# Attention of a four-layer kernel: values and turned probabilities as rounded parts and rests, multiplied in three passes

## The reference

```python
q = (hidden_states @ Wq.T).reshape(b, s, NH, HD).transpose(0, 2, 1, 3)     # NH = 16, HD = 128
k = (hidden_states @ Wk.T).reshape(b, s, NKV, HD).transpose(0, 2, 1, 3)    # NKV = 4
v = (hidden_states @ Wv.T).reshape(b, s, NKV, HD).transpose(0, 2, 1, 3)
scores = jnp.einsum('bhqd,bhkd->bhqk', qf, kf)
scores = jnp.where(causal, scores, neg)
attn = jax.nn.softmax(scores, axis=-1).astype(v.dtype)
out = jnp.einsum('bhqk,bhkd->bhqd', attn, v_rep)
return out.transpose(0, 2, 1, 3).reshape(b, s, NH * HD) @ Wo.T + bo
```

## Time and profile before

| | |
|---|---|
| median of 3 executions | 1227.35 us |
| the profiled execution | 1228.41 us, its span 1226.7 us |
| TensorE busy | 1124.7 us (92% of the span) |
| weight loads, beside it | 963.5 us (79%) |
| VectorE, ScalarE, GpSimd busy | 852.9, 637.3, 211.1 us |
| attention's main loop | about 33 to 469 us of the span |
| granted TensorE clock, mean of the span | 0.927 |

### The profile page before, as it was taken

The page is one execution under the profiler, slowest core; times in us unless marked ns, Lnnn a source line. Parts: engine busy times, 40 slices in busy tenths (PEclk is TensorE's granted clock), DMA queues, the critical chain, the costliest instruction groups (busy, mean ns, idle before and its releaser), DMA issues. The chain is left out here.

```text
span 1226.7 us, 26372 instructions
## 1 busy us (share of the span) xinstructions
PE 1124.7 (92%) x9980; PEld 963.5 (79%) x9980; DVE 852.9 (70%) x2427; ACT 637.3 (52%) x1596; POOL 211.1 (17%) x245
## 2 busy tenths in 40 slices
PE   3999999999999998999999999578799889898888
PEld 2799899889989987888888898456577667776767
DVE  4677567647856776667766757798889779777343
ACT  4654444444444443553444434456788688665341
POOL 0422132222222222430000000200220121021100
PEclk9999999999999998999999999678798798867789
DMA  9020000000000003001000000100000000000034
GB/s 311 2 70 2 1 1 1 1 1 1 2 1 1 1 1 95 1 1 28 1 1 1 1 1 30 57 30 3 32 30 3 31 31 30 3 2 3 25 94 141
DMA packets 26701, 32.90 MB, mean 27 GB/s; under 512 B 4960, under 2 KB 21968, under 8 KB 26576
## 3 DMA queue, kind: packets, MB, share of 16 engines
q1 hardware_dynamic: 24400, 29.12, 7.5%
q10 hardware_dynamic: 2176, 2.10, 0.5%
HBM read 29.04 MB, written 2.17 MB: 25 GB/s over the span
## 5 line engine op out<-in xcount | busy, mean ns | idle before, releaser
L365 DVE TENSOR_TENSOR a_ps<-a_ps,causal 128x256 f32<-128x256 f32 x128 | 54.7, 427 | 100.9 <-PE a_ps L635 100.9
L1537 PE MATMUL b_ps<-ln_high,b_high 128*128 128x512 f32 x256 | 101.6, 397 | 1.0 <-ACT gate_up_raw L1452 1.0
L683 PE MATMUL a_ps<-a_wo_high,a_oT 128*128 128x256 f32 x512 | 101.2, 282 | 0.1
L1537 PE MATMUL b_ps<-ln_low,b_high 128*128 128x512 f32 x256 | 100.8, 394 | 0.0
L1537 PE MATMUL b_ps<-ln_high,b_low 128*128 128x512 f32 x256 | 100.5, 392 | 0.0
L348 POOL TENSOR_TENSOR a_probs<-a_probs,a_inv 128x256 f32<-128x256 f32 x64 | 40.2, 627 | 339.9 <-DVE a_inv L385 339.9
L1571 PE MATMUL b_ps<-b_wd_high,b_mid 128*128 128x256 f32 x512 | 97.8, 286 | 0.0
L508 ACT ACTIVATE a_probs<-a_ps,a_negmax 128x128 f32<-128x128 f32 x128 | 47.1, 368 | 88.8 <-DVE a_negmax L371 79.5
L520 ACT CAST a_oT<-a_ps 128x512 fp32r<-128x512 f32 x64 | 37.5, 587 | 107.1 <-PE a_ps L661 107.1
L1452 ACT ACTIVATE gate_up_raw<-b_ps 128x512 f32<-128x512 f32 x64 | 37.4, 597 | 101.4 <-PE b_ps L1537 101.3
L1337 DVE TENSOR_TENSOR gate_up_raw<-gate_up_raw,b_ps 128x512 f32<-128x512 f32 x64 | 42.8, 685 | 62.8 <-ACT gate_up_raw L1452 34.2
(11 more groups left out here) (438 smaller groups left out, 3101.9 us busy)
## 6 DMA issues: line engine op xcount, KB each, us to landing
gate_up_raw<-a_scratch SPq DMA_DIRECT2D x8, 768.0 KB, 3.6
d_main<-in_D_main SPq DMA_DIRECT2D x14, 304.5 KB
x<-in_hidden SPq DMA_DIRECT2D x4, 512.0 KB, 10.6
a_raw<-in_A_q SPq DMA_DIRECT2D x4, 512.0 KB, 8.3
gate_up_raw<-in_A_o SPq DMA_DIRECT2D x1, 2048.0 KB
gate_up_raw<-in_B_g SPq DMA_DIRECT2D x1, 2048.0 KB, 12.2
gate_up_raw<-in_B_u SPq DMA_DIRECT2D x1, 2048.0 KB, 8.3
out<-x ACTq DMA_DIRECT2D x8, 256.0 KB, 2.2
```

The lines of the kernel that those rows point to most:

```text
L365: nc.vector.tensor_tensor(diagonals, diagonals, r.causal[:].rearrange("p (o k) -> p o k", o=1).to_broadcast([P, 2, P]), ALU.add).then_inc( ...
L683: mm = nc.tensor.matmul(ps[:, out_bank(job), 0:HID], opart, wpart, start=(k == 0 and j == 0), stop=(k == QUARTER - 1 and j == len(passes) ...
L1537: mm = nc.tensor.matmul(ps[:, bank, :], wpart, xpart, start=(j == 0), stop=(j == len(passes) - 1))
```

## The change

The values are kept as `v_high` and `v_low`, the turned probabilities as `pT_high` and `pT_low`. ScalarE writes the high parts, VectorE the low ones. The product of values and probabilities is made by three float32r passes in place of one plain product, for the 256-column part and for the 128-column part alike. The scores stay plain. pT_high and pT_low have one buffer each (before: two of pT), and the queries one (before: two). `v_low` lies where the gate weights of four of the eight experts are loaded to, so the DMA of B_g is split in three: two experts' part in the first block, two experts' part after the output weights are split, and the last four experts' part after the last head's product. The experts' layer waits for all three in ScalarE and in VectorE before it touches these.

```diff
         kT = later[:, 0:NKV * GROUP].rearrange("p (g t) -> p g t", t=GROUP)
-        qT = later[:, NKV * GROUP:(NKV + 2) * GROUP].rearrange("p (s t) -> p s t", t=GROUP)
...
-        v = [half[:, t, :] for half in (v_first, v_rest) for t in range(GROUP_TILES // 2)]
+        qT = later[:, NKV * GROUP:(NKV + 1) * GROUP]
+        v_highs = [by_token(over(x, at, 2 * NKV * HD)) for x, at in (("v_high0", ahead.xn_at),
+                                                                    ("v_high1", kept.xnT_at + (NKV + 2) * TILE))]
+        v_high = [half[:, t, :] for half in v_highs for t in range(GROUP_TILES // 2)]
+        v_lows = by_token(over("v_low", gates_at + PAST_FIRST, GROUP_TILES * NKV * HD))
+        v_low = [v_lows[:, t, :] for t in range(GROUP_TILES)]
...
-        pT = sb("pT", [P, 2, GROUP_BATCHES, QW])
+        pT_high, pT_low = [sb(x, [P, GROUP_BATCHES, QW], F32R) for x in ("pT_high", "pT_low")]
...
-                next_weights.load(sp, 0)
+                next_weights.load(sp, 0, NLORA, NLORA + 2)
...
                 next_weights.load(sp, 1)
                 next_weights.load_router(sp)
+                sp.wait_ge(next_weights.loaded[0], 16)
+                next_weights.load(sp, 0, 0, NLORA)
+                sp.wait_ge(oT_ready, GROUPS * NH)
+                next_weights.load(sp, 0, NLORA + 2, NE)
...
-                def copy_pT(G):
+                def lower_pT(G):
                     for b in range(GROUP_BATCHES):
-                        dve.wait_ge(pT_ready, 2 * G + b + 1)
-                        if G >= 2:
-                            dve.wait_ge(oT_ready, G - 1)
-                        nc.vector.tensor_copy(pT[:, G % 2, b, :], ps[:, PTB[b], 0:QW]).then_inc(pT_copied, 1)
+                        dve.wait_ge(pT_high_done, 2 * G + b + 1)
+                        nc.vector.tensor_tensor(pT_low[:, b, :], ps[:, PTB[b], 0:QW], pT_high[:, b, :].bitcast(F32),
+                                                ALU.subtract).then_inc(pT_copied, 1)
+
+                def lower_v(i, t):
+                    dve.wait_ge(v_high_done, i * GROUP_TILES + t + 1)
+                    nc.vector.tensor_tensor(v_low[t], ps[:, PROJ[t % 2], :], v_high[t].bitcast(F32), ALU.subtract
+                                            ).then_inc(v_taken, 1)
...
+                    if h == 0:
+                        for t in range(GROUP_TILES):
+                            lower_v(i, t)
...
-                    nc.scalar.copy(v[t], ps[:, PROJ[t % 2], :]).then_inc(v_taken, 1)
+                    nc.scalar.copy(v_high[t], ps[:, PROJ[t % 2], :]).then_inc(v_high_done, 1)
+
+                def take_pT(G, b):
+                    act.wait_ge(pT_ready, 2 * G + b + 1)
+                    if G >= 1:
+                        act.wait_ge(oT_ready, G)
+                    nc.scalar.copy(pT_high[:, b, :], ps[:, PTB[b], 0:QW]).then_inc(pT_high_done, 1)
...
-                    if G >= 2:
-                        act.wait_ge(scores_ready, 2 * (G - 1))
-                    nc.scalar.copy(qT[:, G % 2, :], ps[:, PROJ[1], :]).then_inc(q_taken, 1)
+                    if G >= 1:
+                        act.wait_ge(scores_ready, 2 * G)
+                    nc.scalar.copy(qT, ps[:, PROJ[1], :]).then_inc(q_taken, 1)
...
                     exps(G, 0)
+                    if h >= 1:
+                        take_pT(G - 1, 0)
+                        take_pT(G - 1, 1)
                     exps(G, 1)
...
+                    if h == NH - 1:
+                        take_pT(G, 0)
+                        take_pT(G, 1)
...
-                        nc.tensor.matmul(out, v[2 * b][:, g], pT[:, G % 2, b, 0:2 * P], start=True, stop=False)
-                        mm = nc.tensor.matmul(out[:, P:2 * P], v[2 * b + 1][:, g], pT[:, G % 2, b, 2 * P:QW],
-                                              start=False, stop=True)
+                        firsts, seconds = [split_passes(v_high[t][:, g], v_low[t][:, g], pT_high[:, b, cols], pT_low[:, b, cols])
+                                           for t, cols in ((2 * b, slice(0, 2 * P)), (2 * b + 1, slice(2 * P, QW)))]
+                        for j, (vpart, ppart) in enumerate(firsts):
+                            nc.tensor.matmul(out, vpart, ppart, start=(j == 0), stop=False)
+                        for j, (vpart, ppart) in enumerate(seconds):
+                            mm = nc.tensor.matmul(out[:, P:2 * P], vpart, ppart, start=False, stop=(j == len(seconds) - 1))
```

More of the change, by code:

```diff
@@ L24 @@
 LN_EPS = 1e-5
+WORD = 4
 NEG = -1e30
@@ L41, in __init__ @@
         self.first_xnT = sb("first_xnT", [P, DC, GROUP])
+        self.first_xnT_at = nc.sbuf_base - DC * GROUP * WORD
         self.x_loaded = [ctx.enter_context(nc.semaphore(f"x_loaded{g}")) for g in range(GROUPS)]
@@ L103, in __init__ @@
         self.xn = sb("xn", [P, GROUP_TILES, HID])
+        self.xn_at = nc.sbuf_base - GROUP_TILES * HID * WORD
         self.xnT = [first_xnT]
@@ L205, in attention, with over, by_head, by_token @@
         later = kept.xnT[:].rearrange("p c t -> p (c t)")
-        kT = later[:, 0:NKV * GROUP].rearrange("p (g t) -> p g t", t=GROUP)
-        qT = later[:, NKV * GROUP:(NKV + 2) * GROUP].rearrange("p (s t) -> p s t", t=GROUP)
-        v_rest = later[:, (NKV + 2) * GROUP:(NKV + 4) * GROUP].rearrange("p (t n) -> p t n", n=NKV * HD)
-        v_first = ahead.xn[:].rearrange("p t d -> p (t d)").rearrange("p (t n) -> p t n", n=NKV * HD)
-        v = [half[:, t, :] for half in (v_first, v_rest) for t in range(GROUP_TILES // 2)]
+        def over(name, at, words):
+            return nc.alloc_sbuf_tensor_at("a_" + name, [P, words], F32R, offset=at)[:]
+        def by_head(x):
+            return x.rearrange("p (g t) -> p g t", t=GROUP)
+        def by_token(x):
+            return x.rearrange("p (t n) -> p t n", n=NKV * HD)
+        TILE = NKV * HD * WORD
+        gates_at, PAST_FIRST = next_weights.raw_at, (NLORA + 2) * DC * FE * WORD
+        kT = later[:, 0:NKV * GROUP].rearrange("p (g t) -> p g t", t=GROUP)
+        qT = later[:, NKV * GROUP:(NKV + 1) * GROUP]
[4 more added lines that the diff above has]
+        v_low = [v_lows[:, t, :] for t in range(GROUP_TILES)]
         negmax = sb("negmax", [P, 2, GROUP_TILES])
@@ L231, in attention @@
         bias_added, out_ready, out_taken = sem("bias_added"), sem("out_ready"), sem("out_taken")
+        v_high_done, pT_high_done = [sem(x) for x in "v_high_done pT_high_done".split()]
         M = {x: sem("m_" + x) for x in ahead.NAMES.split()}
@@ L456, in _ @@
                     if h >= 1:
-                        copy_pT(G - 1)
+                        lower_pT(G - 1)
                     invert(G)
@@ L473, in _ @@
                     if h == NH - 1:
-                        copy_pT(G)
+                        lower_pT(G)
                         add_out(out_jobs(i, h)[1])
@@ L627, in scores @@
                     pe.wait_ge(k_taken, i * NKV + h // REP + 1)
-                    q, k = qT[:, G % 2, :], kT[:, h // REP, :]
+                    q, k = qT, kT[:, h // REP, :]
                     for b in range(GROUP_BATCHES):
@@ L742, in attention @@
             probs_ready, pT_ready, pT_copied, oT_ready, oT_copied, oT_split, bias_added, out_ready, out_taken,
-            wo_loaded, bo_loaded, wo_rounded, wo_split])
+            wo_loaded, bo_loaded, wo_rounded, wo_split, v_high_done, pT_high_done])
 NE, FE, RANK, NLORA = 8, 256, 64, 2
@@ L832, in __init__ @@
         self.xnT = ctx.enter_context(nc.sbuf_tensor("all_xnT", [P, DC, TOKENS], F32))
+        self.xnT_at = nc.sbuf_base - DC * TOKENS * WORD
         self.a_dram = nc.dram_tensor("a_scratch", [BATCH, DH * SEQ], F32).ap()
@@ L1061, in squares @@
                                      ).then_inc(self.S["square_ready"], 1)
+GATE_PARTS = 3
 class GateUpWeights:
@@ L1069, in __init__ @@
         self.raw = ctx.enter_context(nc.sbuf_tensor("gate_up_raw", [P, 2, NE, DC, FE], F32))
+        self.raw_at = nc.sbuf_base - 2 * NE * DC * FE * WORD
         self.wr = ctx.enter_context(nc.sbuf_tensor("router_w", [P, DC, NE], F32))
@@ L1074, in __init__, with load @@
         self.router_loaded = ctx.enter_context(nc.semaphore("router_loaded"))
-    def load(self, sp, k):
-        sp.dma_start(self.raw[:, k], self.sources[k].rearrange("e (c p) f -> p e c f", p=P)
+    def load(self, sp, k, first=0, end=NE):
+        sp.dma_start(self.raw[:, k, first:end], self.sources[k][first:end].rearrange("e (c p) f -> p e c f", p=P)
                      ).then_inc(self.loaded[k], 16)
@@ L1320, in add_low_rank @@
                 def add_low_rank(job):
+                    dve.wait_ge(gate_up_weights.loaded[0], 16 * GATE_PARTS)
                     k, e = job // NLORA, job % NLORA
@@ L1481, in _ @@
                     if i == 0 and e + 2 < NE:
+                        if e == 0:
+                            act.wait_ge(gate_up_weights.loaded[0], 16 * GATE_PARTS)
                         take_high(0, e + 2)
```

## The result

The changed kernel takes 1232.99 us (median of 20 runs, 1225.18 to 1240.09); the kernel before took 1222.84 us beside it (20 runs). The ratio is 1.0083, 95% interval 1.0056 to 1.0109: 10 us slower, less than 1%. One of the 20 executions of the kernel before, a slow one of 1595.76 us, is left out of the ratio. The prediction's sum was +10.4 us; measured are +10.2. The forecast of 1238 is 5 us off as a time, since its starting point of 1227.35 us, a median of 3, was 4.5 us above that of 20.

The account below looks back on a forecast made before the run. TensorE was taken to bound attention, busy 99.23 of 100 us. Terms 5.1 + 3.6 + 0.8 + 0.9 = 10.4 us over the median of 1227.35 gave about 1238 us; own range 1231 to 1243, full range 1220 to 1260.

Parts of the forecast that it names:

- TensorE's part: Product of values and probabilities in attention: 1.39 us instead of 1.31 per step, +5.1 us in 64 steps.
- (b): Rival: narrow float32r passes are as slow as plain ones, 0.22 us each; about 1275 us, chance 0.12.
- (c): Rival: narrow passes hide their weight load, 0.06 us each; 1222 us, chance 0.08.
- The chain in full steps: ScalarE, VectorE and GpSimd in full attention steps: slack shrinks from 1.5 to 0.65 us, TensorE doesn't wait.
- Rival (a): A new wait in every attention step, from the longer chain; 1247 us, up to 1256, chance 0.18.
- The first group: Steps 1 to 5, where no output job covers the chain: TensorE waits longer, +3.6 us.
- The changes of group: Step 0 of each group, values through ScalarE then VectorE, and step 15's wait for probabilities: +0.8 us.
- The last step: Attention's very last step: nothing covers the exponentials' delay of 0.85 us, +0.9 us.
- Query buffer and DMAs: The single query buffer and the gates' split loads cost nothing.
- Rival (d): The pass count decides: a quarter of the product saved, 21 us less 5 us of waits; 1212 us, chance 0.05.

Follow-up runs that it names:

- e2: The kernel before with values and probabilities rounded and multiplied in three equal passes, no rests made; 1227.19 us, ratio 1.0046 to the kernel before.
- e3: The changed kernel with its narrow passes over 64 columns instead of 128, the other 64 left out; 1232.82 us, ratio 1.0064 to the kernel before.
- e4: The changed kernel with its narrow passes over 256 columns instead of 128, partly the wrong columns; 1235.44 us, ratio 1.0093 to the kernel before.
- e9: The changed kernel with two more ScalarE copies per step, 384 and 128 columns, ahead of the second exponentials; 1247.33 us, ratio 1.0196 to the kernel before.
- e8: The changed kernel with one more ScalarE copy of 384 columns per step, ahead of the second exponentials; 1239.65 us, ratio 1.0114 to the kernel before.
- e7: e5 with the keys projected before the product of values and probabilities in the first group's steps 1 to 3; 1212.43 us, ratio 0.9899 to the kernel before.
- e1: The changed kernel making all rounded parts and rests, but multiplying only the rounded parts, plainly, once; 1228.19 us, ratio 1.0049 to the kernel before.
- e6: The changed kernel with two query buffers again, nothing else; 1233.12 us, ratio 1.0086 to the kernel before.
- e5: The changed kernel with three passes for the 256-column products alone, the 128-column ones plain and unrounded; 1215.97 us, ratio 0.9949 to the kernel before.

## Why the prediction was right, step by step

- **TensorE's part, +5.1 us: right, a little high.** A head's product was to take 1.39 us and takes 1.38; a step 6.15 and takes 6.14 to 6.15. e2 has this term alone: 0.07 us in nearly every step and 4.0 us in all. A narrow pass costs 0.1125 us, between the floor of 0.109 and the 0.114 I took. e3 and e4 settle that it isn't the columns, and the pace of the weight loads, 0.11 us, says what it is. Rivals (b) and (c), 0.22 and 0.06 us a pass, are out. The 0.06 us between the first and the second narrow pass could be taken for (c); the sum to the next group shows that it isn't.
- **The chain in full steps, 0: right, with more room than I counted.** In the changed kernel's timeline of ScalarE, of VectorE and of GpSimd (one fence each, as in the earlier trace rows):

```profile
207.49 0.37 ACT L542 ACTIVATE a_probs<-a_ps,a_negmax 128x128 f32<-128x128 f32 x1 [0.98 <-DVE a_negmax L392]
...
208.30 0.86 ACT L528 CAST a_pT_high<-a_ps 128x384 fp32r<-128x384 f32 x2
209.03 0.40 ACT L542 ACTIVATE a_probs<-a_ps,a_negmax 128x128 f32<-128x128 f32 x1
```

```profile
206.28 0.43 DVE L386 TENSOR_TENSOR a_ps<-a_ps,causal 128x256 f32<-128x256 f32 x1 [0.54 <-PE a_ps L675]
...
208.81 1.02 DVE L398 TENSOR_TENSOR a_pT_low<-a_ps,a_pT_high 128x384 fp32r<-128x384 f32 x2 [0.44 <-ACT a_pT_high L528]
...
212.52 0.41 DVE L464 TENSOR_SCALAR all_xnT<-x,ln_mv,ln_t 128x256 f32<-128x256 f32 x1
212.84 0.42 DVE L386 TENSOR_TENSOR a_ps<-a_ps,causal 128x256 f32<-128x256 f32 x1
```

```profile
210.83 1.04 POOL L371 TENSOR_TENSOR a_probs<-a_probs,a_inv 128x512 f32<-128x512 f32 x1
```

  The two rounded copies take 0.86 us, as I had them, but the second exponentials stand 1.54 us behind the first (207.49 to 209.03) instead of 1.00: 0.54 us later, not 0.85, because ScalarE used to idle about 0.3 us there until VectorE had the second maximum. I added the copies' length to a queue that had a gap. GpSimd ends at 211.87, 5.59 us after the masks began, against 5.01 before; the next turn is due at 206.74 + 6.15 = 212.89, so 1.0 us of room is left instead of the predicted 0.65. e9 agrees: with its copies 0.4 us is left in steps 7 to 11, and steps 7 to 10 don't grow.
  Of VectorE I had written that its slack was nearly used up. In this step it is gone: the masks begin at 212.84, right behind the layer norm, while the scores they wait for are due 6.15 us after the last ones, at 212.43. The masks are 0.4 us late. Nothing comes of it since 0.6 us of the turn's room are left. Rival (a) was so half true, and it did not decide; in e8 and e9, where ScalarE has 0.5 and 0.8 us more to do, it does, in steps 11 to 13.
- **The first group, +3.6 us: right in kind, 1.0 too high.** Steps 1 to 5 grew by 2.95 us, of which five products are 0.07 each: 2.6 us of waits. The waits for probabilities are 1.03, 0.46, 0.55 and 0.55 us in steps 1 to 4 (timeline of TensorE in the changed kernel, 28 to 66 us):

```profile
41.09 0.36 PE L703 MATMUL a_ps<-a_pT_high,a_v_high 128*128 128x256 f32 x1 [1.03 <-DVE a_pT_low L398]
47.92 0.38 PE L703 MATMUL a_ps<-a_pT_high,a_v_high 128*128 128x256 f32 x1 [0.46 <-DVE a_pT_low L398]
54.85 0.36 PE L703 MATMUL a_ps<-a_pT_high,a_v_high 128*128 128x256 f32 x1 [0.55 <-DVE a_pT_low L398]
61.75 0.36 PE L703 MATMUL a_ps<-a_pT_high,a_v_high 128*128 128x256 f32 x1 [0.55 <-DVE a_pT_low L398]
65.14 0.87 PE L685 MATMUL a_ps<-ident,a_probs 128*128 128x128 f32 x6 [0.48 <-POOL a_probs L371]
```

  Step 1 was predicted at 1.35 and grew by 1.09, steps 2 and 3 at 0.7 and grew by 0.56; step 4 at 0.5 (0.54), step 5 at 0.4 (0.19). I had expected the view of waits to show about 8 us; it shows 6.1. That the wait for GpSimd would grow was wrong: in step 5 it is 0.48 us, as the 0.49 of before, and step 4's 0.5 us is a wait for the probabilities instead. That more cover takes these waits away is shown by e7: steps 1 to 3 shrink by 0.6 to 0.7 us.
- **The changes of group, +0.8 us: mis-sized, about 2.6.** Steps 15 to 17 give up to 0.98 us each time, of which three products are 0.2; three changes make 2.3 us, and step 0 another 0.3. Two places:

```profile
141.21 0.39 PE L650 MATMUL a_ps<-a_w_high,ln_high 128*128 128x512 f32 x1
...
142.34 0.39 PE L650 MATMUL a_ps<-a_w_high,ln_low 128*128 128x512 f32 x1
142.77 0.50 PE L650 MATMUL a_ps<-a_w_high,ln_high 128*128 128x512 f32 x1
...
151.64 0.27 PE L705 MATMUL a_ps<-a_pT_high,a_v_low 128*128 128x128 f32 x1
152.02 0.47 PE L618 MATMUL a_ps<-ln_high,a_w_high 128*128 128x512 f32 x1
```

  The first gap is the one I predicted: a tile of values goes through ScalarE and VectorE before its bank is free, 1.56 us (141.21 to 142.77; I had 1.58). But the six passes that should cover it last 1.37 us (0.2275 each), not the 1.47 I took from a queries' projection whose first pass is slow: 0.2 us of wait, twice my 0.1. And the pass behind the wait takes 0.34 us to the next (142.77 to 143.11) instead of 0.23, which I had at nothing: 0.3 us in all, in step 16 as in step 0. The second, 0.38 us between the last pass and the keys' first instead of 0.11, so 0.27 us, I had missed. In step 17 the keys' projection follows the products directly and needs the bank of the output job; VectorE adds that to x last, behind the reciprocal, which waits for the later exponentials. Its addition ends at 151.88. e8's row for line 424 is the same place with 0.5 us. Step 15 has such a place too, of 0.1 us more than before; TensorE's wait for the probabilities there, where I had put 0.1, did not grow (0.76 us, 0.77 before). e1, where only the chain differs from before, grows by 0.93 us in steps 15 to 17, so this loss is the chain's, and the passes' share is mostly hidden in its waits.
- **The last step, +0.9 us: wrong, nearly nothing.** From the last scores to the last turn it is 7.13 us (461.11 to 468.24) against 6.96 (451.33 to 458.29), and the end of attention behind the last scores didn't move (19.58 against 19.56 us to the router's first product, at 480.69 and 470.89). The second exponentials are 0.5 us later, but the reciprocal that needs them stands behind VectorE's rest of the probabilities, and before it stood behind VectorE's copy of them. It begins 5.21 us after the scores (466.32) where it began 5.05 us after them (456.38), so nearly all of the delay is hidden.
- **Query buffer and DMAs, 0: right.** e6 shows it for the buffer. Of the gates' last part no wait is seen in the trace, and the time after attention doesn't follow it (755.0 us in e5 and 742.5 in e9, which both have it); it was not tried by itself.
- **Rival (d),** a quarter of the product less, 1212 us: wrong for the change, and its condition named why (a pass must cost its columns alone). The wide passes come nearer to it: 0.155 us a step predicted from rows, 0.16 measured in e5. By the Trainium skill's rule of four passes for true float32 ("FP8 and Floating Point Precision", TensorE Precision Notes) three passes would save a quarter, an estimate of 0.215 us a step for the wide products (a quarter of 0.86); the trace agrees in the direction and gives three quarters of it, since a pass of 256 columns takes 0.1175 us and not a quarter of 0.43.

The sum was 10.4 us and the measurement 10.2, but part of that is luck: the changes of group were 1.8 us too small, the first group 1.0, the last step 0.9 and TensorE's part 0.8 too large. Between the first and the last scores stand 62 products of 0.07 us, 4.3 us; with 2.6 and 2.6 that makes 9.5, and the scores' span gives 9.4. The prediction had given the largest chance, 0.50, to a loss of over 1%, and 0.44 to a change within 1%, which it was (0.8%).

## What to carry to other kernels

With 128 columns of weights, three float32r passes beat one plain float32 product at 256 columns (0.35 us against 0.43) and lose at 128 (0.34 against 0.22), since each pass pays 0.11 us for its weights. Widths between were not tried. Split the product by width and convert only the wide part (e5: -6 us instead of +10). A longer chain off the busiest engine costs nothing where a step has cover, so look for the steps without it, at the start and at changes of group, and put independent work of the busy engine there (e7, in the first group).

## What the runs showed of the hardware

- The first narrow pass after wide ones leaves a gap of only 0.06 us (128 columns) or 0.03 us (64 columns) to the next, and the pass behind the narrow group takes 0.17 or 0.20 us instead of 0.12, while the weight loads keep about 0.11 us. One interval read by itself gives the wrong price: add up the whole group and the record behind it.
- The first pass of 512 columns after a wait of 0.2 us took 0.34 us to the next instead of 0.23 (step 16 of the changed kernel), so a wait costs more than its gap.
- One ScalarE copy of 384 columns from SBUF took 0.54 us (e8, mean of 56), one from PSUM 0.49 (120 in the changed kernel).
- The same instructions after attention took 755 us at a granted clock of 0.88 in one execution and 749 at 0.89 in another. The changed kernel alone ran from 1225.18 us at a mean clock of 0.941 to 1240.09 at 0.926.
